# DCT plus a six-step convolutional ODE on one core: inner loops written out, PSUM bank pairs rotating, GpSimd's centring behind two powers, transform bursts spread

## The reference

```python
y = jnp.einsum('kh,bchw->bckw', Dh, _gn(x))          # DCT over rows
x = x + jnp.einsum('lw,bckw->bckl', Dw, y)           # and over columns
def odefunc(t, y):
    h = jax.nn.relu(_group_norm(y, gn1_w, gn1_b))
    h = _concat_conv(t, h, conv1_w, conv1_b)         # 3x3, 33 channels in (t is one)
    h = jax.nn.relu(_group_norm(h, gn2_w, gn2_b))
    h = _concat_conv(t, h, conv2_w, conv2_b)
    return _group_norm(h, gn3_w, gn3_b)
y = _gn(x)
for t in 0, 1/6, .., 5/6:  y = y + odefunc(t, y) / 6
return x + y
```

## Time and profile before

| | |
|---|---|
| median of 3 runs | 3929.45 us (3923.02 to 3934.27) |
| profiled execution | 3909.36 us, span 3907.5 us |
| mean granted clock of PE | 0.912 |
| busy, of the span | PE 79%, DVE 69%, ACT 64%, POOL 20% |
| one MID step | 82.1 us |

### The profile page before, as it was taken

How to read it: one execution, slowest core, us unless ns; L and a number is a source line. 1 busy time by engine, 2 the same in 40 slices (tenths; PEclk the granted TensorE clock), 3 DMA queues, 4 the chain that set the end, 5 groups by cost and what they waited for, 6 DMA issues and landing times.

```text
span 3907.5 us, 148776 instructions
## 1 busy us (share of the span) xinstructions
PE 3088.8 (79%) x61716; PEld 2534.1 (65%) x61716; DVE 2692.2 (69%) x6177; ACT 2493.3 (64%) x3867; POOL 771.4 (20%) x1405
## 2 busy tenths in 40 slices
PE   3587788787887887887887888887888887888884
PEld 3566666666676666666666666666666666677773
DVE  6576676667767767676767677767676776767783
ACT  0465568556676667766676566856668665687774
POOL 4022211222122221222212222122211222111111
PEclk7799989989899998999989999889998999999997
DMA  3300023111331131312303213031131211321113
GB/s 79 75 19 19 19 52 86 43 43 43 60 85 43 43 80 24 85 48 80 60 2 96 74 44 60 19 109 43 44 60 44 85 43 43 60 62 50 53 44 100
DMA packets 368749, 217.32 MB, mean 56 GB/s; under 512 B 353152, under 2 KB 353520, under 8 KB 366064
## 3 DMA queue, kind: packets, MB, share of 16 engines
q1 hardware_dynamic: 368112, 207.63, 21.2%
HBM read 104.85 MB, written 77.07 MB: 47 GB/s over the span
## 4 chain that ended last, share of the span: by engine, by line
PE 25%; issue 24%; ACT 19%; DVE 17%; POOL 10%; DMA 1%; SPq 1%; DVEq 0%; POOLq 0%; ACTq 0%
PE cps L1426 20%; ACT z L651 7%; ACT z L681 6%; POOL xn L550 5%; DVE y L1077 3%; ACT hb L680 3%; POOL m L540 2%; PE dps L1534 2%; DVE bni L1114 1%; PE dps L1542 1%; DVE ha L1073 1%; SPq L432 1%; ACT unread_z L671 1%; DVE bn L1122 1%; POOL small L497 1%
## 5 line engine op out<-in xcount | busy, mean ns | idle before, releaser
L1426 PE MATMUL cps<-ha,w 64*64 64x392 f16 (+1 forms) x27648 | 1470.6, 358 | 345.7 <-ACT z L651 194.0
L1426 PEld LDWEIGHTS cps<-ha,w 64*64 64x64 f16 x27648 | 1101.3, 113 | 591.8 <-issue 398.2
L651 ACT ACTIVATE z<-cps,bias_now 128x784 f32<-128x784 f32 (+2 forms) x1056 | 765.1, 740 | 1010.0 <-PE cps L1426 1005.0
L1426 PE MATMUL cps<-hb,w 64*64 64x392 f16 x27648 | 1299.3, 338 | 12.6 <-DVE hb L1073 7.8
L1426 PEld LDWEIGHTS cps<-hb,w 64*64 64x64 f16 x27648 | 1067.7, 109 | 148.5 <-issue 18.3
L497 POOL TENSOR_TENSOR small<-small,half 128x1 f32<-128x1 f32 x304 | 167.7, 552 | 1949.0 <-DVE small L1004 1363.1
L1103 DVE BATCH_NORM_STATS2 bnt<-z 128x6 f32<-128x392 f32 (+1 forms) x768 | 389.6, 550 | 133.7 <-ACT z L651 133.7
L1073 DVE TENSOR_TENSOR ha<-z,ha 128x784 f16<-128x784 f32 x384 | 373.0, 971 | 103.6 <-ACT z L681 100.0
L1073 DVE TENSOR_TENSOR hb<-z,hb 128x784 f16<-128x784 f32 x384 | 375.1, 977 | 92.9 <-ACT z L681 80.8
L681 ACT ACTIVATE z<-y,small 128x784 f32<-128x784 f32 x320 | 326.3, 1031 | 119.8 <-DVE small L1060 119.8
L681 ACT ACTIVATE z<-z,small 128x784 f32<-128x784 f32 x384 | 396.1, 1031 | 0.0
(11 more groups left out here) (161 smaller groups left out, 2631.4 us busy)
## 6 DMA issues: line engine op xcount, KB each, us to landing
xa<-x_dram SPq DMA_DIRECT2D x128, 196.0 KB, 5.0
y<-xa SPq DMA_DIRECT2D x16, 1568.0 KB, 7.5
y_dram<-y SPq DMA_DIRECT2D x128, 196.0 KB, 4.7
xs<-in_x_dram SPq DMA_DIRECT2D x31, 784.0 KB, 9.9
x_dram<-x1s SPq DMA_DIRECT2D x30, 784.0 KB, 5.9
fin<-y_dram SPq DMA_DIRECT2D x30, 784.0 KB, 9.4
fin<-x_dram SPq DMA_DIRECT2D x28, 784.0 KB, 8.3
out_dram<-fin SPq DMA_DIRECT2D x28, 784.0 KB, 4.4
```

The source lines that it names most:

```text
L651: return nc.scalar.activation(dst, src, ACT.Identity, bias=bias_now[parts, conv:conv + 1], **more)
L1426: return pe.matmul(dst, w[hin * 64:(hin + 1) * 64, kx, a, wl, :], src[:, :, 0:NA], start=(what == "X" and n == 0), stop=(what == "Y" and n ...
```

## The change

1. The inner loops over s are written out on PE, ACT, DVE and POOL, and so is the loop over the last group's steps; SP keeps its loop. The rows of the programs go from 1140 to 2496 (PE), 1011 to 1768 (DVE), 437 to 890 (ACT) and 236 to 412 (POOL).
2. The bank pair is (1 + s + phase + k) % 3, so that pairs rotate through phases and steps, and the lag is 3 everywhere.
3. On POOL the centring of a MID stands behind the powers of Z2,0 and Y,0, with a wait for its own end behind it; the half image's own power stays ahead of them.
4. The four pairs of transform bursts go from (1,0) (2,0), (3,0) (4,0), (5,0) (6,0), (7,0) (8,0) to (1,0) (1,9), (3,2) (3,10), (5,0) (5,8), (6,4) (8,0).
5. Statistics Z2,0 in phase 2 at (1,8) instead of (1,3), Z2,1 in phase 3 at (1,5) instead of (1,3), `half_mean` in phase 1 at (6,0) instead of (3,0).
6. On DVE `half_post` stands one product later, and phase 3 is ordered anew with added(3) last. On ACT phase 3 is ordered anew.

```diff
@@ -77,11 +77,17 @@
 LO_ROW = 32
 
 
+
 PHASES = (("X", 0), ("X", 1), ("Y", 0), ("X", 2), ("Y", 1), ("X", 3), ("Y", 2), ("Y", 3))
-PAIR_BANKS = ((0, 1, 2, 0), (1, 2, 0, 1), (2, 0, 1, 2), (2, 0, 1, 2))
-PAIR_LAG = ((3, 3, 3, 3), (3, 3, 3, 3), (3, 3, 3, 3), (1, 4, 4, 3))
+PAIR_LAG = 3
+
+DCT_ROUNDS = (((1, 0), (1, 9)), ((3, 2), (3, 10)), ((5, 0), (5, 8)), ((6, 4), (8, 0)))
 TOP, BOTTOM, COLUMN = 0, NA, 2 * NA
 RIM = 2 * NA + R + 1
+
+
+def pair_bank(s, phase, k):
+    return (1 + s + phase + k) % 3
 
 
 def dct_matrix():
@@ -550,6 +556,7 @@
                     last = nc.gpsimd.tensor_scalar(xn[:, c, :], xs[:, c, :], m0[:, 4, c:c + 1],
                                                    m0[:, 6, CQ + c:CQ + c + 1], ALU.mult, ALU.add)
                 last.then_inc(xn_done, 1)
+                pool.wait_ge(xn_done, n - HALVES + 1)
 
             def setup():
@@ -598,7 +605,6 @@
                 wrap_rows(1, conv_at(g, s, 2), fixes + 1, pows)
                 if kind == MID:
                     half_rsqrt(HALVES * (g + 1) + s, m0)
-                    normalise_half(HALVES * (g + 1) + s)
                 if kind == FIVE:
                     rsqrt_of(IY, 0)
                 rsqrt_of(Z2, 0)
@@ -606,6 +612,8 @@
                     rsqrt_of(Z2, 1)
                     return
                 pows = rsqrt_of(*((IY, 1) if kind == FIVE else (Y, 0)))
+                if kind == MID:
+                    normalise_half(HALVES * (g + 1) + s)
                 seam(0, conv_at(g, s, 3), fixes + 2, pows)
                 pows = rsqrt_of(Z2, 1)
                 if kind != FIVE:
@@ -615,11 +623,11 @@
                     rsqrt_of(IZ, 0)
 
             with pool.Fori(0, GROUPS - 1) as g:
-                with pool.Fori(0, HALVES) as s:
+                for s in range(HALVES):
                     step(g, s, MID)
                 step(g, 4, FOUR)
                 step(g, 5, FIVE)
-            with pool.Fori(0, STEPS - 1) as s:
+            for s in range(STEPS - 1):
                 step(GROUPS - 1, s, LAST_MID)
             step(GROUPS - 1, 5, LAST)
@@ -642,10 +650,10 @@
                 nc.scalar.activation(rim_now[:, conv, :], rim, ACT.Identity).then_inc(bias_set, 1)
                 act.wait_ge(bias_set, 2 * n + 2)
 
-            def evacuate(slot, conv, phase, k, c):
+            def evacuate(slot, conv, s, phase, k, c):
 
                 act.wait_ge(pair_done, NP * c + k + 1)
-                at = 2 * BANK * PAIR_BANKS[phase][k]
+                at = 2 * BANK * pair_bank(s, phase, k)
@@ -818,27 +826,27 @@
                         batch_copy(b, NBATCH * hn + b, dps)
 
                 copied(0)
-                evacuate(0, 0, 3, 0, c)
+                evacuate(0, 0, s, 3, 0, c)
+                copied(1)
                 state_part(1, 0, True)
-                copied(1)
                 state_part(1, 1, True)
-                evacuate(0, 0, 3, 1, c)
+                evacuate(0, 0, s, 3, 1, c)
                 copied(2)
                 state_part(1, 2, True)
-                evacuate(0, 0, 3, 2, c)
+                state_part(1, 3, True)
                 copied(3)
-                evacuate(0, 0, 3, 3, c)
-                state_part(1, 3, True)
+                evacuate(0, 0, s, 3, 2, c)
+                evacuate(0, 0, s, 3, 3, c)
                 if kind == FIVE:
                     final_state(1, 0)
                     final_state(1, 1)
 
             with act.Fori(0, GROUPS - 1) as g:
-                with act.Fori(0, HALVES) as s:
+                for s in range(HALVES):
                     step(g, s, MID)
@@ -1301,8 +1309,6 @@
                 split_for(2, 0)
                 split_for(2, 1)
                 products_of(1, 1)
-                if kind == MID:
-                    half_post(hn, stats_before(g, s, kind) + STATS[MID].index((X0, 0)))
                 if kind == FIVE:
                     post_of(IY, 0)
                 if kind == FOUR:
@@ -1313,6 +1319,8 @@
                     dve.wait_ge(ibn_done, SLOTS * (g + 1) + 1)
                     pre_of(IZ, 0, 7)
                 products_of(1, 2)
+                if kind == MID:
+                    half_post(hn, stats_before(g, s, kind) + STATS[MID].index((X0, 0)))
                 split_for(2, 3)
                 products_of(1, 3)
@@ -1343,37 +1351,38 @@
                             dve.wait_ge(x1_out, 16 * first_place(hn) + 16)
                         half_add(b, NBATCH * hn + b, dps)
 
-                update(1, lambda: euler(1, 0))
+                update(1, (lambda: added(0)) if kind == MID else lambda: euler(1, 0))
+                if kind == MID:
+                    euler(1, 0)
+                stats_of(3, 0)
                 euler(1, 1)
+                split_for(4, 0)
+                added(1)
                 euler(1, 2)
-                added(0)
-                stats_of(3, 0)
-                split_for(4, 0)
-                euler(1, 3)
-                added(1)
                 split_for(4, 1)
                 stats_of(3, 1)
-                added(2)
+                euler(1, 3)
                 split_for(4, 2)
                 if kind == MID:
                     with dve.If(g > 0):
                         last_add(g * HALVES + s)
                 if adds:
                     last_add(g * HALVES + s)
+                added(2)
+                split_for(4, 3)
                 stats_of(3, 2)
+                stats_of(3, 3)
                 added(3)
-                stats_of(3, 3)
-                split_for(4, 3)
                 if kind == FOUR:
                     post_of(IZ, 0)
                     start_stats(1, g + 1, range(7))
 
             with dve.Fori(0, GROUPS - 1) as g:
-                with dve.Fori(0, HALVES) as s:
+                for s in range(HALVES):
                     step(g, s, MID)
                 step(g, 4, FOUR)
@@ -1493,13 +1502,13 @@
                         if k == NP - 1 and conv == 0:
                             pe.wait_ge(fix_done, c + 1)
                         if not first:
-                            pe.wait_ge(evac_done, NP * c + k + 1 - PAIR_LAG[phase][k])
+                            pe.wait_ge(evac_done, NP * c + k + 1 - PAIR_LAG)
                         elif k == NP - 1:
                             pe.wait_ge(evac_done, 1)
-                        elif k == 2:
+                        elif k == 1:
                             pe.wait_ge(x1_done, NBATCH * HALVES + 1)
 
-                    conv_phase(slot, conv, c, PAIR_BANKS[phase][k], what, k,
+                    conv_phase(slot, conv, c, pair_bank(s, phase, k), what, k,
@@ -1594,38 +1603,38 @@
                 between = {(1, 8): lambda: statistics_of(Z1, 0)}
                 if kind == FIVE:
                     between[5, 0] = lambda: statistics_of(IZ, 1)
-                convolve(1, 0, 0, conv_at(g, s, 0), sets, between)
+                convolve(1, 0, s, 0, conv_at(g, s, 0), sets, between)
 
                 between = {(1, 8): lambda: statistics_of(Z1, 1)}
                 if kind == MID:
-                    between[3, 0] = lambda: half_mean(hn, stats_before(g, s, kind) + STATS[MID].index((X0, 0)))
+                    between[6, 0] = lambda: half_mean(hn, stats_before(g, s, kind) + STATS[MID].index((X0, 0)))
                 if kind == FIVE:
                     between[5, 0] = lambda: statistics_of(IY, 0)
-                convolve(0, 1, 1, conv_at(g, s, 1), sets + 1, between)
-
-                between = {(1, 3): lambda: statistics_of(Z2, 0)}
+                convolve(0, 1, s, 1, conv_at(g, s, 1), sets + 1, between)
+
+                between = {(1, 8): lambda: statistics_of(Z2, 0)}
                 if kind == FIVE:
                     between[6, 0] = lambda: statistics_of(IY, 1)
-                convolve(1, 1, 2, conv_at(g, s, 2), sets + 1, between)
+                convolve(1, 1, s, 2, conv_at(g, s, 2), sets + 1, between)
 
                 if kind == LAST:
                     statistics_of(Z2, 1)
                     return
-                between = {(1, 3): lambda: statistics_of(Z2, 1)}
+                between = {(1, 5): lambda: statistics_of(Z2, 1)}
                 if kind == MID:
-                    for b in range(NBATCH):
-                        between[1 + 2 * b, 0] = lambda b=b: rows_of(b)
-                        between[2 + 2 * b, 0] = lambda b=b: dct_columns(b, NBATCH * hn + b, dps)
+                    for b, at in enumerate(DCT_ROUNDS):
+                        between[at[0]] = lambda b=b: rows_of(b)
+                        between[at[1]] = lambda b=b: dct_columns(b, NBATCH * hn + b, dps)
                 if kind == FOUR:
                     between[8, 0] = lambda: statistics_of(IZ, 0)
-                convolve(0, 0, 3, conv_at(g, s, 3), sets + 2, between)
+                convolve(0, 0, s, 3, conv_at(g, s, 3), sets + 2, between)
 
             with pe.Fori(0, GROUPS - 1) as g:
-                with pe.Fori(0, HALVES) as s:
+                for s in range(HALVES):
                     step(g, s, MID)
                 step(g, 4, FOUR)
```

(2 more changed lines are left out.)

34 lines of the change are left out of this document (17 added, 17 removed).

## The result

| | before | changed |
|---|---|---|
| median of the runs | 3929.2 us (3923.02 to 3934.27) | 3807.97 us (3801.98 to 3808.72) |
| profiled execution | 3909.36, span 3907.5 | 3808.01, span 3806.2 |
| mean granted clock | 0.912 | 0.916 |
| ratio | | 0.9689, 95% interval 0.9672 to 0.9706 |

The change takes 3.1%, 121 us, from the median. 3838 was forecast, with 3590 to 3940 as the range. Against the forecast for that execution, 3818, the changed kernel's 3808 is 10 less; the other 20 lie in which execution of before was profiled.

What follows compares the result with a forecast made beforehand. No engine is full; PE, 79% busy, stands still some 17 us of an 82.1 us MID. Gains of 76 in seven groups and 15 in the last, -91, take 3909.4 to 3818, plus 20 for the median: 3838; range 3590 to 3940.

Steps and rivals of the forecast that it cites:

- S: Zero point of a MID's times: PE's statistics matmul of Z2 for slot 0, at 1242.04 in the profile before.
- The new wait: PE in phase 3, before X1: waits 7.6 us for the centring's xn in place of the 6.58 stall; gain 0.
- Written-out loops: PE's idle of 2.48 us at the top of the loop goes, at 21 tops inside the groups.
- Rival C: Written-out code must be fetched, 1.96 us in each of 56 phases: 3948 us; slower, by this above all, chance 0.12.
- T: Start of the next phase 0 on PE, forecast 43.6 us after the Z2,0 statistics instead of 46.6.
- The load of the next half image: SP's load, issued after added(3), lands 57.5 us after the Z2,0 statistics; DVE waits 3.4 us for it.
- D: Rival: the next half image's load lands earlier, no 3.4 us DVE wait, 71 us more, 3767; within the forecast's 0.50.
- S': The next step's Z2,0 statistics, forecast 80.1 us after this one's: gain 2.0 (82.1 to 80.1), three times a group.
- The fourth MID: Last MID of a group, followed by a step without half image, no loop top: gains 0.5 + 0.6 = 1.1 us.
- FOUR, FIVE, the last group: Other steps: FOUR gains 2.8 us and FIVE 1.0, 7 times each; LAST_MID gains 3.0, 5 times.
- A: Rival: the centring hides beside DVE, PE never waits for xn, MID period 71.2 us, 3588 us; below 3650, chance 0.17.
- E: Rival: rotating banks do not free phase 3, as evacuations are late; 35 us don't come, 3873; within the forecast's 0.50.

Runs made afterwards that it cites:

- the split: Changed kernel with half_mean and half_post early, 5 centring channels ahead of the Z2,0 power and 11 behind the Y,0 power: 3766.12 us, ratio 0.9618.
- the added matmuls: Changed kernel with 28 matmuls that compute nothing needed, right before PE's wait for xn: 3731.32 us, ratio 0.9516.

## Why the prediction was right

Up to the statistics Z2,1 its path was right nearly to the microsecond in a MID of groups 1 to 6; its sum was right partly by errors that cancel. For the profiled execution it had -91 and got -101: the first three MIDs of a group gave 74 where it had 42, and the fourth ones, FOUR, FIVE and the last group together 22 where it had 49; the rest came ahead of the first mark. It took one MID of period 82.2 for all; their mean before, in groups 1 to 6, was 83.3.

- **The stall ahead of phase 3.** Forecast gone, L1045 at S+1.8, X0 done at S+12.9. Measured S+1.75, X0's first matmuls at S+10.0 and its end at S+12.6. Right.
- **The new wait.** Forecast xn at S+20.5, a wait of 7.6, L1031 at S+24.0, gain 0. Measured S+19.9, 7.4, S+23.9, and "MID, in" +0.2. Right in sum. The working was not: of "one channel in at each of 11 joints; each costs DVE 0.25" the rows show 7 channels and a loss to DVE of 0.4 in all, not 2.7. DVE keeps its pace, and more channels are left for the end. The two errors cancelled; in the split, whose expectation rested on a mean price for each channel, they didn't, and it missed by 76 us. (S+17.6, 2.2 and 0.98 also add up to S+20.8, not 20.5; and by 0.43 a joint in place of 0.25 the end comes 2.0 later, S+22.5, and costs 56 us, not 42.)
- **Gain 0 by the idle, not by the clock.** The same stall length at another place costs more. The forecast put half clock on five rounds behind the wait (1.9, where full clock takes 1.0); the added matmuls show 77 us, 2.8 a MID. Undoing the move gains 75 with everything else kept, 80 with `half_mean` and `half_post` back too. In the kernel before, the move alone gained 35 to 54. So what the move is worth depends on what stands around it. What turns the sign was not tried, and the two traces of the move alone don't show its gain in the MIDs.
- **Written-out loops.** The term was mis-sized: 2.5 at 21 places, in part lost to the load; measured 89 us alone, since 1.3 of half clock goes with each. In the changed kernel no run took the loops out by themselves; all its "MID, out" fell by 3.1 in groups 1 to 6, where the loops alone gave 4.2. Rival C falls: marked "issue" PE idles 41 us ahead of its `ha` matmuls in the changed kernel, where it was 88.
- **The end of phase 3.** Spreading the bursts was to shorten the stretch from L1031 to there from 20.3 to 19.6; it took 21.0 (1220.45 to 1241.45), with 1.85 of waiting for the third add in it. So T came at S+44.9, not 43.6, and the last add ended at S+47.3, not 46.0. No run undid the spreading, so what it is worth by itself isn't shown.
- **The load of the next half image.** Forecast: DVE waits 3.4. Measured 1.86 and 1.41 in two MIDs, 0.9 in group 0, 1.4 in the mean of groups 1 to 6. It landed 9.2 after its issue, not 10.7; with SP's rows:

```profile
1244.55 1.24 SPq L369 DMA_DIRECT2D xs<-in_x_dram  x1
```

```profile
1253.73 0.81 DVE L1130 BATCH_NORM_STATS2 bn<-xs 112x6 f32<-112x112 f32 x4 [1.86 <-DMA xs<-in_x_dram]
```

  The mechanism of D came half true. The earlier landing made up for the later T, and the load was there at S+57.2 (forecast 57.5). S' was forecast at S+80.1 and came at S+79.3.
- **The fourth MID** was to gain 1.1 and lost 1.2 a group. Behind it is FOUR, in which DVE is the bound, and PE waits for it:

```profile
1441.30 0.39 PE L1529 MATMUL sps<-zsum,mats 128*128 128x12 f32 x2 [4.58 <-DVE unread_yz L1093]
```

  A phase 3 that ends with DVE's last add makes DVE later there. I argue this from the order of the rows; no run undid the order alone.
- **FOUR, FIVE, the last group**: forecast -20, -7, -15; measured -14, -9, -8. In the last group the start of phase 3 was earlier by the 3.0 (S+9.4 after S+12.6), but "in" gained 1.0: PE waits 1.55 for DVE's products ahead of Z2,1 there.
- **Rivals A and E** held as mechanisms. A appeared with reads taken away (L1030 at S+16.4, period 69.7 in the mean of groups 1 to 6). Its forecast had T at S+34.9, 1.2 earlier than its own S+16.5 and 19.6 give, and even so the time came 62 us below its 3588. E, that the banks are worth nothing, agrees with the medians beside the wait for xn and is false without it.

## What to carry to other kernels

Price a wait together with the half clock behind it, and ask what PE does in the microseconds after it: filling one wait with useless matmuls gave back 2%. POOL's 8, 11 or 16 operations that read SBUF, put beside a full DVE queue of operations with two inputs, all ended behind that queue, and each one fewer saved only 0.4 to 0.5 us. Put such work where DVE waits, or give it to ACT. And test parts of a change in each other's presence: here the banks were worth nothing that could be told or 79 us, and the centring's move -75 or +35 to 54, by what stood beside them.
